# Single blocks' rows and five blocks' weights loaded ahead into places of their own

## The reference

```python
xn = _layernorm(x)
s = _L0_attn_ref(xn, ...)            # 16 heads of 64, null keys, alibi, causal
g = _silu(_L0_ffn_ref(xn, ...))      # top-1 of 8 experts
x = x + s * g
xn = _layernorm(x)
s = _L1_attn_ref(xn, ...)            # one head of 128, causal
g = _silu(_L1_ffn_ref(xn, ...))      # top-2 of 8 experts, at most CAP rows each
x = x + s * g
...
# an expert, on the rows that chose it
h = jax.nn.gelu(rows @ W1[e] + b1[e], approximate=False)   # 128 -> 512
out = h @ W2[e] + b2[e]                                    # 512 -> 128
```

## Time and profile before

| what | value |
|---|---|
| median of three runs | 1045.22 us |
| profiled execution, span of its instructions | 1043.3 us (the profile has no other time of that execution) |
| PE busy | 961.4 us, 92% |
| DVE, ACT, POOL busy | 692.3, 630.9, 650.4 us |
| layer 0's experts on PE | 312 to 397 us |
| layer 1's experts on PE | 867 to 1014 us |
| DMA busy over 895 to 910 us | 0.82 |

### The profile page before, as it was taken

How to read it: one execution, slowest core, us unless ns; L and a number is a source line. 1 busy time by engine, 2 the same in 40 slices (tenths; PEclk the granted TensorE clock), 3 DMA queues, 4 the chain that set the end, 5 groups by cost and what they waited for, 6 DMA issues and landing times.

```text
span 1043.3 us, 21426 instructions
## 1 busy us (share of the span) xinstructions
PE 961.4 (92%) x6330; PEld 690.3 (66%) x6330; DVE 692.3 (66%) x2589; ACT 630.9 (60%) x1945; POOL 650.4 (62%) x803
## 2 busy tenths in 40 slices
PE   5699989999999979999999999999998999999965
PEld 2465546666658976666665665666666788999954
DVE  6988867886673335867768768677885474345634
ACT  4458857667664557677676775766765564444442
POOL 4663787888855544667776678788746651555540
PEclk9889999999999999999999999999999999999997
DMA  9300202202427783033032030331232134787759
GB/s 296 79 7 6 42 27 66 71 26 64 113 74 188 221 233 84 10 72 81 6 66 50 22 71 26 73 67 41 52 82 52 34 102 143 227 229 226 219 168 242
DMA packets 95444, 103.19 MB, mean 99 GB/s; under 512 B 10096, under 2 KB 83031, under 8 KB 95089
## 3 DMA queue, kind: packets, MB, share of 16 engines
q1 hardware_dynamic: 88752, 89.36, 33.5%
q0 software_dynamic: 6592, 12.65, 3.5%
HBM read 77.54 MB, written 23.50 MB: 97 GB/s over the span
## 4 chain that ended last, share of the span: by engine, by line
PE 54%; DVE 18%; ACT 7%; POOL 7%; issue 6%; DMA 3%; SPq 3%; DVEq 0%; POOLq 0%; ACTq 0%
PE bank L1347 9%; PE bank L823 8%; PE bank L834 7%; PE bank L1376 7%; PE bank L1403 5%; DVE arena L2032 5%; PE bank L1391 4%; ACT arena L1759 4%; PE bank L1366 3%; PE bank L1426 3%; DVE arena L2041 3%; POOL arena L1130 2%; DVE arena L1932 2%; POOL expert_rows L655 2%; DMA arena<-in_b 1%
## 5 line engine op out<-in xcount | busy, mean ns | idle before, releaser
L1759 ACT ACTIVATE arena<-arena 128x128 f32<-128x128 f32 (+1 forms) x512 | 226.9, 446 | 96.7 <-DVE arena L2032 96.5
L2032 DVE CUSTOM_DVE_ANT_0 arena<-bank,arena 128x128 f32<-128x128 f32 (+1 forms) x512 | 183.0, 412 | 107.1 <-PE bank L1376 104.4
L1347 PE MATMUL bank<-arena 128*128 128x512 f32 x384 | 211.1, 636 | 6.0 <-ACT arena L1748 3.6
L1130 POOL TENSOR_TENSOR arena<-arena 128x512 f32<-128x512 f32 x128 | 133.4, 1045 | 121.7 <-ACT arena L1735 104.1
L2041 DVE COPY arena<-bank 128x384 f32<-128x384 f32 x256 | 130.0, 549 | 21.1 <-PE bank L1391 20.9
L1145 POOL TENSOR_TENSOR arena<-arena 128x512 f32<-128x512 f32 x128 | 129.5, 1048 | 1.3
L1735 ACT ACTIVATE arena<-bank 128x512 f32<-128x512 f32 x192 | 112.7, 588 | 27.8 <-PE bank L1347 27.5
L1391 PEld LDWEIGHTS bank<-const,arena 128*128 128x128 f32 x768 | 91.3, 142 | 56.0 <-issue 55.0
L784 POOL DMA_INDIRECT expert_out<-arena x71 | 71.1, 1002 | 90.0 <-DVE arena L923 42.1
L1376 PE MATMUL bank<-arena 64*128 64x128 f32 (+1 forms) x1024 | 119.3, 351 | 2.2 <-DVE arena L2032 1.5
L1403 PE MATMUL bank<-arena 128*64 128x256 f32 (+1 forms) x1024 | 112.2, 340 | 9.1 <-DVE arena L2041 8.7
(11 more groups left out here) (304 smaller groups left out, 1634.1 us busy)
## 6 DMA issues: line engine op xcount, KB each, us to landing
arena<-in_wp SPq DMA_DIRECT2D x40, 514.0 KB
arena<-recip_rows SPq DMA_DIRECT2D x30, 512.0 KB, 6.4
XN<-in_wp SPq DMA_DIRECT2D x24, 514.0 KB
arena<-expert_rows SPq DMA_DIRECT2D x46, 129.0 KB, 3.2
arena<-in_b SPq DMA_DIRECT2D x64, 64.0 KB
arena<-expert_out SPq DMA_DIRECT2D x16, 256.0 KB, 5.1
expert_out<-fill SPq DMA_DIRECT2D x11, 338.6 KB, 7.9
expert_rows<-fill SPq DMA_DIRECT2D x1, 2644.5 KB, 21.6
```

The source lines that it names most:

```text
L1130: pool.tensor_tensor(sq[:, i % 2], r, r, ALU.mult).then_inc(S["sq_done"], 1)
L1347: mm = pe.matmul(RING[bnk][:, :], xa[:, p, t * P:(t + 1) * P], wqkv[:, 512 * k:512 * k + 512], start=True, stop=True)
L1759: ins = act.activation(w, w, ACT.Exp, bias=nm[:, p, 16 * t + h:16 * t + h + 1], scale=-1.0, accum_out=den[:, p, 16 * t + h:16 * t + h + 1])
L2032: ins = v.tensor_tensor_reduce(out=SPb[:, c % 2, 384 * k + P * t:384 * k + P * t + n], in0=SBANK[k][:, P * t:P * t + n], in1=alibi[:, h, N ...
```

## The change

- Layer 0's nine single blocks get their rows from `load_single` as well, in steps 4 to 12 (`ROWS_AT`), into `SROWS0`, places of their own in a buffer that the attention left. `turn` of a single waits for all nine.
- One weight place is added in layer 0, for block 19, loaded in step 13 (`OWNW`, `OWN_AT`); four are added in layer 1, for blocks 35 to 38, each loaded by `load_own` in the last step of one of the first four rounds (steps 3, 7, 11 and 15). Blocks past them use the four old places in turn: a place that would have gone to block 19 goes to block 20 and so on, and in layer 1 block 39's weights follow block 31 in its place.
- Layer 1's loop on SP has four rounds in place of five, and single rows 4 to 8 are loaded in steps 16 to 20.
- The 256 rows of a double block are laid out so that partition p holds rows 2p and 2p+1 (one run of 1032 bytes) where it held rows p and p+128 (two runs of 516 bytes). The numbers travel with the rows, so the results go to the same tokens.
- Semaphores that nothing used are dropped.

```diff
+OWNW = ((19,), (35, 36, 37, 38))
+def weight_slots():
+    slots, turns, used = [], [], []
+    for layer in range(2):
+        n, own = NBIG[layer] + NSMALL, OWNW[layer]
+        slot = [j % 4 if j < own[0] else 4 + j - own[0] if j in own else (own[0] + j - own[-1] - 1) % 4 for j in range(n)]
+        slots.append(tuple(slot))
+        turns.append(tuple(sum(slot[m] == slot[j] for m in range(j)) for j in range(n)))
+        used.append(tuple(sum(x == q for x in slot) for q in range(4)))
+    return slots, turns, used
+WSLOT, WTURN, WUSED = weight_slots()
+OWN_AT = ((13,), ())
+ROWS_AT = range(4, 4 + NSMALL)
...
+        def weights_there(eng, layer, j, q, i):
+            if isinstance(j, int):
+                q, i = WSLOT[layer][j], WTURN[layer][j]
+            if q >= NBUF:
+                eng.wait_ge(S["own_w_in"], 32 * (len(OWNW[0]) + layer * len(OWNW[1])))
+            else:
+                eng.wait_ge(S[f"w_in{q}"], (i + (layer * WUSED[0][q] + 1)) * 32)
...
-                src = xe[layer][bass.ds(row, n * BLK), :].rearrange("(t p) d -> p t d", p=P)
+                src = xe[layer][bass.ds(row, n * BLK), :].rearrange("(p t) d -> p t d", t=n)
...
             def load_single(k):
-                at_ = k + NBIG[1]
-                row = sp.value_load(rowtab[1][0:1, bass.ds(at_, 1)], min_val=0, max_val=NOROWS)
-                dst = SROWS[:, k] if isinstance(k, int) else SROWS[:, bass.ds(k, 1)].rearrange("p k d -> p (k d)")
-                sp.dma_start(dst, xe[1][bass.ds(row, BLK), :]).then_inc(S["single_rows"], 16)
+                at_ = k + NBIG[layer]
+                row = sp.value_load(rowtab[layer][0:1, bass.ds(at_, 1)], min_val=0, max_val=(NOROWS0, NOROWS)[layer])
+                dst = SINGLE[layer][:, k] if isinstance(k, int) else SINGLE[layer][:, bass.ds(k, 1)].rearrange("p k d -> p (k d)")
+                sp.dma_start(dst, xe[layer][bass.ds(row, BLK), :]).then_inc(S["single_rows"], 16)
+            def load_own(k):
+                at_ = k + OWNW[1][0]
+                e = sp.value_load(owner[0:1, bass.ds(at_, 1)], min_val=0, max_val=E - 1)
+                sp.dma_start(OWN1W[:, bass.ds(k, 1)].rearrange("p k d -> p (k d)"), W[bass.ds(e, 1)].rearrange("e p n -> p (e n)"))\
+                  .then_inc(S["own_w_in"], 16)
+                sp.dma_start(OWN1B2[:, bass.ds(k, 1)].rearrange("p k d -> p (k d)"), B2[bass.ds(e, 1)].to_broadcast([P, D]))\
+                  .then_inc(S["own_w_in"], 16)
...
             def step(j, q, i, more=True):
                 sp.wait_ge(S["ye_evac"], j + (base + 1))
-                load_weights(j + NBUF, q, i + 1)
+                if not isinstance(j, int) or j + NBUF < OWNW[layer][0]:
+                    load_weights(j + NBUF, q, i + 1)
+                elif OWNW[layer][-1] + 1 + j + NBUF - OWNW[layer][0] < nblk:
+                    load_weights(OWNW[layer][-1] + 1 + j + NBUF - OWNW[layer][0], q, 0)
+                if isinstance(j, int) and j in OWN_AT[layer]:
+                    load_weights(OWNW[layer][OWN_AT[layer].index(j)], 0, 0)
                 if layer and q == 1 and not isinstance(j, int):
                     load_single(i)
+                if layer and q == 3 and not isinstance(j, int):
+                    load_own(i)
                 if layer and isinstance(j, int) and last <= j < last + NSMALL - last // NBUF:
                     load_single(j - last + last // NBUF)
-                if more and not (layer and single(1, j + NBUF + 2 if isinstance(j, int) else j, q)):
+                if not layer and isinstance(j, int) and j in ROWS_AT:
+                    load_single(j - ROWS_AT[0])
+                if more and not single(layer, j + NBUF + 2 if isinstance(j, int) else j, q):
                     sp.wait_ge(S["xT_evac"], j + (base + 3))
                     load_rows(j + NBUF + 2, (q + 2) % NBUF, i + (q + 2 + NBUF) // NBUF)
...
-            last = (PERIOD[layer][1] - NBUF - 1) // NBUF * NBUF
+            last = (4, 4 * len(OWNW[1]))[layer]
...
             def turn(j, q, i):
-                if layer and single(1, j, q):
-                    pe.wait_ge(S["single_rows"], NSMALL * 16)
-                    mm = pe.transpose(XT[q % 2][:, 0:P], SROWS[:, j - NBIG[1], 0:D], ident)
+                if single(layer, j, q):
+                    pe.wait_ge(S["single_rows"], (layer + 1) * NSMALL * 16)
+                    mm = pe.transpose(XT[q % 2][:, 0:P], SINGLE[layer][:, j - NBIG[layer], 0:D], ident)
                 else:
                     pe.wait_ge(S[f"rows_in{q}"], (i + (counts[q] + 1)) * 16)
-                    for t in range(1 if single(layer, j, q) else 2):
+                    for t in range(2):
                         mm = pe.transpose(XT[q % 2][:, t * P:(t + 1) * P], xb[:, q, t, 0:D], ident)
                 mm.then_inc(S["xT_full"], 1)
...
             def up(j, q, i):
                 pe.wait_ge(S["xT_evac"], j + (base + 1))
-                pe.wait_ge(S[f"w_in{q}"], (i + (counts[q] + 1)) * 32)
+                weights_there(pe, layer, j, q, i)
+                wb = weights(layer, j, q)
```

More of the change, by code:

```diff
@@ L181, in block_kernel @@
         sq = take(2 * 512).rearrange("p (i n) -> p i n", i=2)
-        spare = take(1600)
+        sq_end = at[0]
+        spare = take(1600)[:, WCOLS - 2 * DFF:1600]
         qT = take(2 * HC * N).rearrange("p (i c n) -> p i c n", i=2, c=HC)
@@ L300, in block_kernel @@
         th = RA[:, SIZES[5] + SIZES[6]:SIZES[5] + SIZES[6] + 4 * D].rearrange("p (i n) -> p i n", i=2)
+        assert NSMALL * ROW + len(OWNW[0]) * D <= 2 * 768
+        PTf = PTb[:, :, :].rearrange("p i n -> p (i n)")
+        nown1 = len(OWNW[1])
+        assert nown1 * (WCOLS + D) <= 4096 + 1024
+        OWN_W = ([arena[:, sq_end - 2 * DFF:sq_end - 2 * DFF + WCOLS]],
+                 [arena[:, k * WCOLS:(k + 1) * WCOLS] for k in range(nown1)])
+        SROWS0 = PTf[:, 0:NSMALL * ROW].rearrange("p (k d) -> p k d", k=NSMALL)
+        SINGLE = (SROWS0, SROWS)
+        OWN_B2 = ([PTf[:, NSMALL * ROW + k * D:NSMALL * ROW + (k + 1) * D] for k in range(len(OWNW[0]))],
+                  [arena[:, nown1 * WCOLS + k * D:nown1 * WCOLS + (k + 1) * D] for k in range(nown1)])
+        OWN1W = arena[:, 0:nown1 * WCOLS].rearrange("p (k d) -> p k d", k=nown1)
+        OWN1B2 = arena[:, nown1 * WCOLS:nown1 * (WCOLS + D)].rearrange("p (k d) -> p k d", k=nown1)
         LG0 = OT1[:, :, :].rearrange("p c n -> p (c n)")
@@ L702, in sender, with weights, bias2 @@
             return f"sent{min(place(layer, j, q), NBUF)}"
+        def weights(layer, j, q):
+            if isinstance(j, int):
+                q = WSLOT[layer][j]
+            return OWN_W[layer][q - NBUF] if q >= NBUF else FFNB[layer][0][:, q]
+        def bias2(layer, j, q):
+            if isinstance(j, int):
+                q = WSLOT[layer][j]
+            return OWN_B2[layer][q - NBUF] if q >= NBUF else FFNB[layer][1][:, q]
+        def weights_there(eng, layer, j, q, i):
+            if isinstance(j, int):
+                q, i = WSLOT[layer][j], WTURN[layer][j]
[3 more added lines that the diff above has]
+                eng.wait_ge(S[f"w_in{q}"], (i + (layer * WUSED[0][q] + 1)) * 32)
         def sends(layer, j, q, i):
@@ L713, in ffn_sync @@
             W, B2 = a[f"wp_{layer}"], a[f"b2_{layer}"]
-            wb, b2b, xb = FFNB[layer][0:3]
+            xb = FFNB[layer][2]
             def load_rows(j, q, i):
@@ L735, in step @@
+                sp.dma_start(weights(layer, j, q), W[bass.ds(e, 1)].rearrange("e p n -> p (e n)")).then_inc(S[landed], 16)
+                sp.dma_start(bias2(layer, j, q), B2[bass.ds(e, 1)].to_broadcast([P, D])).then_inc(S[landed], 16)
             def step(j, q, i, more=True):
                 sp.wait_ge(S["ye_evac"], j + (base + 1))
-                load_weights(j + NBUF, q, i + 1)
+                if not isinstance(j, int) or j + NBUF < OWNW[layer][0]:
+                    load_weights(j + NBUF, q, i + 1)
+                elif OWNW[layer][-1] + 1 + j + NBUF - OWNW[layer][0] < nblk:
+                    load_weights(OWNW[layer][-1] + 1 + j + NBUF - OWNW[layer][0], q, 0)
@@ L823, in up @@
                     mm = pe.matmul(HB[2 * (q % 2) + c // 2][:, (c % 2) * DBL:(c % 2) * DBL + n],
[L824 removed]
+                                   wb[:, c * P:(c + 1) * P], xbT[:, q % 2, 0:n], start=True, stop=True)
                 mm.then_inc(S["h_full"], 1)
@@ L860, in ffn_scalar @@
             HB = HBANKS[layer]
-            wb, hT = FFNB[layer][0], FFNB[layer][3]
+            hT = FFNB[layer][3]
             def gelu(j, q, i):
@@ L865, in gelu @@
                 act.wait_ge(S["h_full"], j + (base + 1))
-                act.wait_ge(S[f"w_in{q}"], (i + (counts[q] + 1)) * 32)
+                weights_there(act, layer, j, q, i)
+                wb = weights(layer, j, q)
                 n = BLK if single(layer, j, q) else DBL
@@ L902, in ffn_vector @@
             XT, YB = bank[0:2], bank[6:8]
-            _, b2b, xb, _, xbT, _, _ = FFNB[layer]
+            _, _, xb, _, xbT, _, _ = FFNB[layer]
```

(4 more changed lines are left out.)

24 lines of the change are left out of this document (12 added, 12 removed).

## The result

The changed kernel took 1052.73 us (median of 7 runs, 1050.97 to 1059.78) against 1045.22 before (7 runs, 1040.76 to 1048.38): ratio 1.0073, interval 1.0044 to 1.0101. By the ratio that is 7.6 us slower. The interval lies above 1, so the loss is real, but it is within the 1% that was called no change. The forecast was +2.7 us. The measured time lies in the range of 1040 to 1054 that was to hold in 8 of 10 cases, and 0.7 us outside the forecast's own range of 1043 to 1052.

A forecast was written before the change was run, and what follows sets the result against it. Double blocks were taken as bound by TensorE, single blocks by weight loads. 4.3 + 2.0 - 3.9 + 0.8 - 0.5 = +2.7 us on 1045.2 gave 1047.9 us; own range 1043 to 1052, 8-in-10 range 1040 to 1054.

The forecast's parts named there:

- The stall at turn(15): Layer 0: TensorE waits for the ninth single row, a new stall of 6.4 us (5.7 to 7.4).
- Part 2, the clock: Layer 0, step 13: the stall lowers TensorE's granted clock, +2.0 us (0 to 3.6).
- The rival in which the clock holds: Layer 0: the stall does not lower the clock; +0.7 us in all, 1045.9 us; chance 0.20.
- Part 1, what comes back: Layer 0 after the stall: blocks at 2.56 us each recover some, leaving +4.3 us (+0.6 to +6.4).
- a sign that I had named for being wrong: Layer 0: up(18) to up(23) following at under 2.2 us would show the prediction wrong.
- The rival in which the loads keep up: Layer 0's last six blocks pass at TensorE's pace: +0.6 there, total -1.0, 1044.2 us; chance 0.15.
- Part 3, the tail of layer 1: Layer 1's single blocks: weights already in place, steps of 1.94 us, -3.9 us (-3.0 to -4.5).
- Part 4, what the double blocks pay: Layer 1's double blocks: four own loads +0.8 us (0 to 9.2); paired rows -0.5 (0 to -2.4).
- falls behind for a step and catches up: SP in layer 1: an own load adds 1.64 us to one step in four, and SP recovers.
- The rival of the scatters: Layer 1: own loads delay scatters, DVE's copy and TensorE; double blocks +9.2, total +11.1, 1056.3 us; chance 0.10.
- another sign that I had named for being wrong: Layer 1: TensorE waiting for DVE's line 915 copy in rounds of own loads would show the prediction wrong.
- The pairing: Paired rows of double blocks shorten at most TensorE's waits on DVE, -0.5 us (0 to -2.4).

The follow-up runs named there:

- warm: The changed kernel with 44 transposes of a constant ahead of turn(15), to keep TensorE busy; ratio to the kernel before 1.0045.
- rows0_only: The kernel before with only layer 0's nine single rows loaded in steps 4 to 12, no own weight places, rows unpaired; ratio to before 1.0067.
- own1_flat: The kernel before with layer 1's four own weight places and SP's steps of layer 1 written out; ratio to before 0.9988.
- best2: The changed kernel, SP's steps written out, both layers' rows in steps 0-8, block 19's weights in 14, layer 1's own loads in 10, 14, 18, 22; ratio to before 0.9993.
- own1_flat_small: As own1_flat, but each own load fetches only 16 of 1028 columns, so results are not the reference's; ratio to the kernel before 0.9974.
- early_rows: The changed kernel with layer 0's nine single rows issued two a step in steps 4 to 8; ratio to the kernel before 1.0029.

## Why the prediction came out as it did

The number came out inside the range, but not because the sum was right: layer 0 cost 1.3 us more than forecast and layer 1 gave 3.2 us less, and both missed the same way. That the total still lies in the range is owed to its width.

- **The stall at turn(15): right.** turn(15) comes 60.6 us behind the first turn against 53.9, 6.7 later; forecast 6.4. 5.5 us of it stand as one wait for the ninth row, issued in SP's step 12 and landed 2.7 us later, where 3.4 had been taken; the rest, 1.2 us, came up before it, and is within the scatter.
- **Part 2, the clock: right, shown by warm.** Step 13 took 5.62 against 3.62 us, +2.0, at a granted clock of 0.50, and 3.69 us where TensorE was kept busy. The rival in which the clock holds is out.
- **Part 1, what comes back: half.** From turn(15) to the last down it took 30.36 us against 29.47, +0.9; less the clock's 2.0 that is -1.1, where I had -2.1. The step that failed here is block 19's own place: the prediction treated it as relief for SP and not as a load that goes ahead of one needed sooner. up(18) waited 3.98 us for weights queued behind it, and the clock fell once more (0.57 over 388 to 392 us). Without that place (rows0_only) the same sum gives 28.77 - 29.47 - 2.0 = -2.7, and up(17) to up(23) followed at 2.52 us each, as in the forecast's 2.56. The rate in the changed kernel was better than I took: in 380 to 390 us 302 GB/s at a share of 0.98, so 658 kB (weights and scatter) in 2.1 us, not 2.56. From up(20) on the steps are 1.9 us, where under 2.2 was a sign that I had named for being wrong (over up(18) to up(23) the mean is 2.2). The rival in which the loads keep up was right for these last blocks, too late to win anything. The rate in the fit of the Trainium skill (DMA: Bandwidth & Descriptors, "Anatomy of one DMA"), 1.4 us for 592 kB, was not reached in these rows. That section gives the fit for DMAs that GpSimd issues, and these loads are SP's, so the prediction used it outside its case. Layer 0 in all: +7.56, forecast +6.3.
- **Part 3, the tail of layer 1: right.** -3.9 us (28.6 to 24.7), as worked out.
- **Part 4, what the double blocks pay: this step failed.** It had +0.8 for the own loads and -0.5 for the pairing, +0.3 in all. The stretch grew by 3.56 us, and by 4.5 with the own loads alone. The sentence that failed is that SP "falls behind for a step and catches up": it priced SP's steps in the loop at the 2.76 us of a written-out step of layer 0, and they take 3.3, so that a round with own weights takes 16.3 us and not less than TensorE's 14.9. The rows to see it, SP's issues in layer 1's loop, were in the trace before and I didn't read them. The rival of the scatters had a mechanism that the runs bear out in part, and too high a price: with SP out of the way each own load is followed by a late copy on DVE (in five of eight cases behind a wait of 2.5 us or more for a scatter), and costs TensorE 0.4 to 1.0 us in own1_flat, up to 1.9 in best2, not 2.3 each time. That TensorE waits for this copy more often, six times for 2.4 us where it had been twice for 0.9, was another sign that I had named for being wrong. Nor did the DMA share reach 0.98 in those rounds; it went from 0.83 to 0.89. The two limits overlap, since removing the bytes alone gives nothing and SP's loop alone 1.3 us (within the scatter), both 2.7.
- **The pairing: nothing measurable**, 1.0013 (0.9986 to 1.0041).

By stage: forecast +6.3 in layer 0 and -3.6 in layer 1, measured +7.6 and -0.4.

## What to carry to other kernels

A load that is moved ahead is paid for in the stretch that it moves into. Before calling it covered, write down the issuing engine's round there from that stretch's own rows: a loop's rows for a loop, and not those of written-out code. A wait for all of a set moves every consumer behind the last member, so the last one's issue time is the price, together with the clock that the idle engine loses. A load that goes early must not stand in the queue ahead of one that is needed sooner.

## What the runs showed of the hardware

- The same step of SP (two weight transfers, one row transfer) costs 3.3 us or more in a register-driven loop and 2.8 at the least written out: 902.66 to 905.98 in the kernel before is 3.32, has 2.76 in layer 0, and in own1_flat_small two plain steps of layer 1 began 2.76 us apart (966.21 and 968.97). With a single's row on top it is 4.2 in the loop and 3.86 to 3.90 in own1_flat (steps 17 to 20).
- Idle times shorter than the stall also lowered the granted clock, but not each time: after 3.98 us of idle the eight matmuls of up(18) took 1.44 us against 1.06, the eight of down(17) behind them 1.92, and the clock of 388 to 392 us was 0.57; in early_rows, after 2.47 us, up(18) took 2.05 at a clock of 0.50 (383 to 386 us); in warm, after 2.76 us, it took 1.13 at 1.00. So the length of the wait alone does not tell.
- With weights alone in SP's queue (and five scatter instructions of GpSimd beside them) the DMA engines moved 302 GB/s at a share of 0.98, against 244 at 0.95 in the earlier trace rows with two row loads and four scatter instructions. These are one window each, and that the row loads make the difference is not shown.
